# Cross attention: the second transpose of maxima goes to the output projection's PSUM bank in the periods that have no output projection, and its negation goes ahead of slot 8's exponential

## The reference

```python
q = _split_heads(query @ wq.T + bq, B)
k = _split_heads(value @ wk.T + bk, B)
v = _split_heads(value @ wv.T + bv, B)
scores = jnp.einsum('bhqd,bhkd->bhqk', q, k) / scale
attn = jax.nn.softmax(scores, axis=-1)
ctx = jnp.einsum('bhqk,bhkd->bhqd', attn, v)
return ctx.transpose(0, 2, 1, 3).reshape(B, -1, D_MODEL) @ wo.T + bo
```

## The kernel before

| slot | uses on PE in order, with the bank |
|---|---|
| 7 | max 20: 4, key 2: 5 |
| 8 | max 0: 7, out: 4 (even periods alone), turn 1: 5 |
| 9 | max 1: 7, max 2: 4, max 3: 5, weigh, max 4: 7 |

## Time and profile before

### The profile page before, as it was taken

The page is one execution under the profiler, slowest core; times in us unless marked ns, Lnnn a source line. Parts: engine busy times, 40 slices in busy tenths (PEclk is TensorE's granted clock), DMA queues, the critical chain, the costliest instruction groups (busy, mean ns, idle before and its releaser), DMA issues.

```text
span 596.3 us, 16647 instructions
## 1 busy us (share of the span) xinstructions
PE 523.4 (88%) x6368; PEld 432.4 (73%) x6368; DVE 392.1 (66%) x768; ACT 314.9 (53%) x488; POOL 293.2 (49%) x219
## 2 busy tenths in 40 slices
PE   3699997799999999999999999999999824999990
PEld 1566673477788788788788788788788623998980
DVE  4867568767787787787787787787786530532331
ACT  2467565265765766666666666665756410333320
POOL 4584426476557457457457457357211072232331
PEclk9899998799999999999999999999999855999996
DMA  9600007498375475475475575574482031455623
GB/s 371 223 3 2 1 3 158 80 193 193 98 168 140 108 163 136 114 159 136 117 156 135 122 155 131 127 155 125 85 213 52 2 102 49 141 183 172 213 85 119
DMA packets 32911, 75.86 MB, mean 127 GB/s; under 512 B 15308, under 2 KB 18892, under 8 KB 32788
## 3 DMA queue, kind: packets, MB, share of 16 engines
q1 hardware_dynamic: 31464, 72.42, 48.5%
q0 software_dynamic: 1408, 2.90, 1.4%
HBM read 33.52 MB, written 8.75 MB: 71 GB/s over the span
## 4 chain that ended last, share of the span: by engine, by line
PE 63%; ACT 4%; issue 4%; SPq 4%; DMA 3%; POOL 3%; DVE 1%; ACTq 0%; POOLq 0%
PE PS L1811 14%; PE PS L1795 13%; PE PS L1771 12%; PE PS L1958 8%; PE PS L244 5%; PE PS L1970 4%; ACT k_full L258 2%; ACT P L1370 2%; POOL slots L1307 2%; PE PS L1824 2%; SPq L1144 1%; SPq L1151 1%; PE PS L1826 1%; PE PS L1825 1%; DMA tokens<-slots 1%
## 5 line engine op out<-in xcount | busy, mean ns | idle before, releaser
L1463 DVE TENSOR_REDUCE chunk_max<-PS 128x1 f32<-128x500 f32 x336 | 212.5, 673 | 59.7 <-PE PS L1771 59.6
L1370 ACT ACTIVATE P<-PS 125x896 f32<-125x896 f32 x192 | 172.6, 917 | 129.6 <-PE PS L1795 127.6
L1771 PE MATMUL PS<-k_hi,q_block_hi 128*128 128x500 f32 x336 | 130.3, 439 | 3.2 <-DVE chunk_max L1463 0.9
L267 POOL TENSOR_TENSOR k_lo<-k_full,k_hi 128x500 fp32r<-128x500 f32 x48 | 60.5, 1263 | 133.0 <-ACT k_full L258 133.0
L1795 PE MATMUL PS<-q_stack,k_stack 97*125 97x224 f32 x768 | 121.1, 281 | 2.1 <-ACT P L1370 1.9
L1795 PEld LDWEIGHTS PS<-q_stack,k_stack 97*125 97x125 f32 x768 | 108.9, 190 | 15.8 <-ACT P L1370 6.2
L1811 PE MATMUL PS<-P,values 125*32 125x112 f32 x3072 | 85.1, 263 | 0.8 <-issue 0.7
L1811 PEld LDWEIGHTS PS<-P,values 125*32 125x32 f32 x3072 | 73.3, 111 | 15.2 <-issue 12.3
L1771 PEld LDWEIGHTS PS<-k_hi,q_block_hi 128*128 128x128 f32 x336 | 62.2, 196 | 22.7 <-DVE chunk_max L1463 9.3
L1330 POOL DMA_INDIRECT parts<-results,tokens x28 | 26.8, 958 | 62.4 <-ACT results L1413 58.1
L244 PE MATMUL PS<-mats,ctxT 128*125 128x128 f32 x384 | 49.9, 273 | 0.0
(11 more groups left out here) (201 smaller groups left out, 681.8 us busy)
## 6 DMA issues: line engine op xcount, KB each, us to landing
k_stack<-k_hi SPq DMA_DIRECT2D x128, 187.5 KB, 4.8
ctxT<-ctx_in SPq DMA_DIRECT2D x16, 750.0 KB, 4.3
k_stack<-k_lo SPq DMA_DIRECT2D x64, 187.5 KB, 4.5
w_gate_up<-wgu_in SPq DMA_DIRECT2D x10, 512.0 KB, 3.9
slots<-slots_in SPq DMA_DIRECT2D x1, 5070.0 KB
w_down<-wd_in SPq DMA_DIRECT2D x10, 256.0 KB, 4.1
more_gate_up<-wgu_in SPq DMA_DIRECT2D x4, 512.0 KB, 3.9
tokens<-slots SPq DMA_DIRECT2D x14, 130.0 KB, 4.0
```

Of the source, the lines that this page charges most:

```text
L267: nc.gpsimd.tensor_tensor(k_lo[:, j, k], k_full[:, k], k_hi[:, j, k].bitcast(F32), ALU.subtract).then_inc(k_lo_ready, 1)
L1370: nc.scalar.activation(P[:, t % RING, :].rearrange("p (a n) -> p a n", a=2), PS[0:KR, 2 * (t % 2):2 * (t % 2) + 2, 0:HALF], ACT.Exp).then_ ...
L1463: nc.vector.tensor_reduce(out=chunk_max[:, n // KC, n % KC:n % KC + 1], in_=PS[:, max_bank(b, n), 0:KW], axis=AX.X, op=ALU.max).then_inc(m ...
L1771: nc.tensor.matmul(PS[:, max_bank(b, n), 0:KW], q_block_hi[:, j, 128 * t:128 * t + 128], k_hi[:, j, KW * c:KW * c + KW], start=True, stop= ...
```

## The change

For a = 1 in odd periods (the transposed batch is then even, so its j is 0) the transpose is written to the bank of "out", 4, in place of 5. In the same periods ACT negates it ahead of exponential 8 and no longer behind it. Everything else, even periods too, stays as it was. Period 0 is even, though it has no output projection either, and keeps bank 5.

```diff
-            def turn_bank(b, a):
-                return bank("turn", a) if later(b, 1) else MISC
+            def turn_place(j, a):
+
+                return BANK_OF["out", 0] if a == 1 and j == 0 else BANK_OF["turn", a]
+
+            def turn_bank(b, j, a):
+                return PS[:, turn_place(j, a), :] if later(b, 1) else MISC
...
                     def period(b, j, u):
                         for t in range(KT):
+                            early = j == 1 and t == TURN_SLOTS[1]
+                            if exists(b + 1, B) and early:
+                                negate_rows(b + 1, 1 - j, u + 1, 1)
                             exps(b, t)
...
-                            if exists(b + 1, B) and t in TURN_SLOTS:
+                            if exists(b + 1, B) and t in TURN_SLOTS and not early:
...
-                    def turn_max(b, a):
+                    def turn_max(b, j, a):
 
                         pe.wait_ge(max_ready, 2 * b + a + 1)
                         if later(b, 1):
-                            take_bank(BANK_OF["turn", a], (rows_ready, 2 * b + a + 1))
+                            take_bank(turn_place(j, a), (rows_ready, 2 * b + a + 1))
                         elif a == 1:
                             pe.wait_ge(rows_ready, 1)
-                        nc.tensor.transpose(turn_bank(b, a)[:, 0:128], max_turn[:, a, :], C["ident"]).then_inc(max_turned, 1)
+                        nc.tensor.transpose(turn_bank(b, j, a)[:, 0:128], max_turn[:, a, :], C["ident"]).then_inc(max_turned, 1)
```

More of the change, by code:

```diff
@@ L1363, in negate_rows @@
                         r = slice(0, HALF_TILES[a].stop - HALF_TILES[a].start)
-                        nc.scalar.mul(neg_rows[r, j, a, :], turn_bank(b, a)[r, 0:128], -1.0).then_inc(rows_ready, 1)
+                        nc.scalar.mul(neg_rows[r, j, a, :], turn_bank(b, j, a)[r, 0:128], -1.0).then_inc(rows_ready, 1)
                     def exps(b, t):
@@ L1842, in _ @@
                         if n == HALF_TILES[0].stop * KC + 5:
-                            turn_max(0, 0)
-                    turn_max(0, 1)
+                            turn_max(0, 0, 0)
+                    turn_max(0, 0, 1)
                     for index in TURNING_BANKS:
@@ L1916, in period @@
                             if exists(b + 1, B) and t in TURN_SLOTS:
-                                turn_max(b + 1, TURN_SLOTS.index(t))
+                                turn_max(b + 1, 1 - j, TURN_SLOTS.index(t))
                             if exists(mb, B):
```

## The result

The changed kernel takes 0.9947 of the time of the kernel before (95% interval 0.9928 to 0.9967; 20 runs of each), 0.53% less: 598.1 us against 601.2 us. The forecast was 594.4 us, 0.5% less, in a range from 592.6 to 597.4 us. The ratio came true. The absolute time didn't and lies above the range, because the kernel before has a median of 601.2 over 20 runs (the three shown are among them), not the 597.38 of those three. 0.9947 of 597.38 would be 594.2.

What follows compares the result with a forecast made beforehand. The prediction took PE, busy for 88% of the span, as the bound. Of a 0.91 us wait, 0.43 us would be gained in 7 odd periods, 3.0 us in all: 597.38 - 3.0 = 594.4 us, range 592.6 to 597.4.

Steps and rivals of the forecast that it cites:

- The wait costs 0.91 us an odd period: Slot 8 of odd periods: PE's transpose of maxima waits for `k_full` though its data is ready; 0.91 us a period.
- Chunk 1 is late next: Behind the transpose, chunk 1 waits for DVE to empty bank 7 of chunk 0; 0.43 us of 0.91 is gained.
- The restart of 0.11: At chunk 1, a matmul starting together with its weight load delays the next by 0.11 us more; without it, 0.54 gained.
- Max 2's wait for the negation costs nothing: Chunk 2 takes bank 4 after the negation, seen by PE at 339.31 to 339.37; margin 0.01 to 0.07 us, cost nothing.
- The negation ahead of exponential 8 costs nothing: On ACT, exponential 8 starts 0.15 to 0.20 us behind the negation; PE needs it 2.0 us later, so no cost.
- Nothing is given back: From chunk 1 on, DVE and ACT follow PE and POOL bears 0.43 us less, so 7 periods keep 3.0 us.
- 597.38 - 3.0 = 594.4: Whole kernel: median of the runs, 597.38 us, less 3.0 us; 1 us more on each side for the median's movement.
- A: Rival at chunk 1: chunk 0's bank is no bound, whole wait goes, 591.0 us; chance 0.12 together with the no-restart case.
- B: Rival: gain given back by a second wait in the period, say max 2 on a late negation; 597.4 us, chance 0.10.
- C: Rival: ACT waits for a late transpose, holding exponentials 8 and 9 back; 600.7 us, chance 0.04.

Runs made afterwards that it cites:

- e3: Changed kernel, but DVE reduces only 250 of chunk 0's 500 columns in odd periods; ratio to the kernel before 0.9945, spacing 44.47 us.
- e4: Changed kernel with one of slot 9's four blocks of products with the values ahead of chunk 1 in odd periods; ratio to before 0.9924, spacing 44.44 us.
- e1: Changed kernel with the negation put back behind exponential 8, so the bank part alone; ratio to before 1.0041, spacing 45.30 us.
- e2: Changed kernel with the transpose put back to bank 5, so the early negation alone; ratio to before 0.9998, spacing 45.06 us.
- e6: Changed kernel with chunk 16 of the maxima moved from slot 4 to behind slot 5's scores in every period; ratio to before 0.9922, spacing 44.27 us.
- e10: Rerun of changed kernel plus one block's products ahead of chunk 1 (odd periods) and chunk 16 behind slot 5's scores; ratio to before 0.9869, spacing 44.11 us.

## Why the prediction was right, and where it was wrong

- *The wait costs 0.91 us an odd period, the change takes it off.* Right: the 7 waits are gone, and the transpose starts 0.24 us behind chunk 0.
- *Chunk 1 is late next, behind DVE's reduction of chunk 0, and 0.43 us of 0.91 remain.* Right. The slots show 2.49 - 2.06 = 0.43, the table's spacing 0.48; e3 shows that it is the reduction. Of the 0.05 between them, 0.02 belongs to period 13, where the table's measure ends: chunk 16 starts 0.11 sooner there in both kernels, and only in the kernel before does slot 8's transpose make up for it with a longer wait (0.82, 0.70 in period 9). From period 3 to 11 the gain is 0.46 a pair. The 0.03 left is not explained.
- *The restart of 0.11, against the weight loads pulled ahead of which the Trainium skill tells (TensorE: Matmul & The Clock Gate, Step-by-step: what each phase is for).* The measurement decides for the row: three chunks take 0.95 and not 0.85, and the weight load of chunk 1 starts with its matmul at 340.07. Yet the row it was read from, 342.25, stands behind products with the values and not behind a wait. There too the weight load starts with its matmul, and e4's chunks show the same 0.94 with no wait. The size was right; that a wait costs it could not be read from that row. The reading given ahead of the rows, that a matmul whose weight load stands at the same start waited, fails there for the same reason.
- *Max 2's wait for the negation costs nothing.* Right in the changed kernel, by a narrow margin: the negation ends at 340.06, and with the 0.11 of e1 and e3 chunk 2's weight load could start at 340.17; it starts at 340.24. e3 shows the rest: 0.27 us less at chunk 1 and the negation is the bound.
- *The negation ahead of exponential 8 costs nothing.* Right; e2 shows it with four times the delay.
- *Nothing is given back.* Right for the periods. 7 x 0.43 = 3.0 was the sum; it is 7 x 0.46 = 3.2 by the pairs inside the loop, and 3.2 by the ratio (0.53% of 601.2).
- *597.38 - 3.0 = 594.4, with 1 us on each side for the median.* **This is the step that failed: the base of the sum.** What was subtracted was right (3.0 us, 3.2 measured), what it was subtracted from wasn't. The step took the median of three runs as the kernel's, and 1 us as the movement of such a median. The same kernel had 601.2 over the 20 runs of the comparison, 3.8 us more, and about 600 on each of the later occasions (599.77 to 600.47); single runs lie between 594.41 and 604.38. On the base of 601.2 the sum gives 598.2, and 598.1 was measured. The three runs shown were from the low side. The range should have been put around a time that may itself be 3 to 4 us off.

The time of one kernel goes in large part with the clock. In the 82 later runs of the kernel before, the mean granted clock lies between 0.939 and 0.961, and a line laid through times and clocks has 3.0 us less for each 0.01 more, with 1 us of scatter left. The clock row of the page before (40 slices of 14.9 us, tenths of full speed) shows where it is low: 8 from 15 to 30 us, 8 and 7 from 89 to 119, 8, 5 and 5 from 462 to 507, and 6 in the last slice.

```profile
PEclk9899998799999999999999999999999855999996
```

Why the three first runs lay low stays open. No clock is on record for them, and the profiled execution had 0.948, the mean of the 82.

Of the rivals, A, B and C didn't happen. e1 is a relative of B: there the negation is late, and the whole gain and 0.24 us more are lost each odd period.

## What to carry to other kernels

When banks or buffers go in turn, list for each use when the one before is released, in order of time, and not only for the use that waits: a removed wait is worth the distance to the next release (here 0.43 of 0.91, in e6 0.31 of 0.70). A buffer freed sooner may need a second edit that is worth nothing alone: the bank without the early negation was slower, the negation without the bank did nothing. And where a gain of half a per cent lies in a loop, measure it by the distance of equal instructions in the trace; forecast a ratio, and widen an absolute time by what the kernel's runs show over many occasions.

## What the runs showed of the hardware

- A wait of PE ends 0.05 to 0.06 us behind DVE's or ACT's instruction in most rows. Behind the negation it is 0.11 for the weight load (e1, e3) and up to 0.15 for the matmul (e1).
- One more change from full matmuls of 500 columns to those of 32 rows of output in column tiles and back costs about 0.3 us in all, with no wait near it (e4: products 1.81 for 1.67, three chunks 0.86 for 0.77, and 0.07 ahead of the block).
- The same first 40 us ran at mean granted clocks from 0.77 to 1.00, between the levels of 1.2 and 2.4 GHz. The first transpose of maxima started between 105.60 and 110.25 us (e6, e10), up to 4.65 us apart, more than the change brings. The Trainium skill (TensorE: Matmul & The Clock Gate, What's actually happening) says that the point at which the clock rises varies from run to run. These traces agree that the same code meets a different clock in each execution (0.89, 0.77 and 1.00 from 10 to 40 us).
